# Cross-attention in a decoder layer: where in the slot the scores for a pair of maxima are made

## The reference, cut to what matters

```python
q = (x @ Wq).reshape(B, N, HEADS, hd).transpose(0, 2, 1, 3)
k = (context @ Wk).reshape(B, M, HEADS, hd).transpose(0, 2, 1, 3)
v = (context @ Wv).reshape(B, M, HEADS, hd).transpose(0, 2, 1, 3)
scores = jnp.einsum('bhid,bhjd->bhij', q, k) * scale
scores = jnp.where(context_mask[:, None, None, :], scores, max_neg)
attn = jax.nn.softmax(scores, axis=-1)
out = jnp.einsum('bhij,bhjd->bhid', attn, v)
return out.transpose(0, 2, 1, 3).reshape(B, N, DIM) @ Wo
```

## Time and profile before

| | us |
|---|---|
| median of 3 runs | 3547.63 |
| lowest and highest of them | 3544.5, 3549.58 |
| profiled execution, its own time | 3545.49 |
| its span in the profile | 3543.5 |
| PE busy in the span | 3231.4 |
| DVE busy | 2578.8 |
| ACT busy | 2275.1 |
| POOL busy | 1072.4 |

### The profile page before, as it was taken

How to read it: one execution, slowest core, us unless ns; L and a number is a source line. 1 busy time by engine, 2 the same in 40 slices (tenths; PEclk the granted TensorE clock), 3 DMA queues, 4 the chain that set the end, 5 groups by cost and what they waited for, 6 DMA issues and landing times.

```text
span 3543.5 us, 47102 instructions
## 1 busy us (share of the span) xinstructions
PE 3231.4 (91%) x15056; PEld 2496.3 (70%) x15056; DVE 2578.8 (73%) x4060; ACT 2275.1 (64%) x4138; POOL 1072.4 (30%) x1177
## 2 busy tenths in 40 slices
PE   5999999999999999978999999988989999941998
PEld 4777777777777878755666666655768888831887
DVE  5887877777777777656788787778863369976554
ACT  4776767676666767644777777766432256678765
POOL 1233232333233333343556555557500000000000
PEclk9999999999999999989999999999999999975999
DMA  3443444434334433336666666655722268889764
GB/s 119 159 160 116 125 144 125 128 116 147 119 125 131 134 114 121 105 116 119 105 112 125 118 116 118 124 100 165 237 77 102 107 220 297 294 338 395 271 243 182
DMA packets 269954, 555.47 MB, mean 157 GB/s; under 512 B 28024, under 2 KB 105856, under 8 KB 255376
## 3 DMA queue, kind: packets, MB, share of 16 engines
q1 hardware_dynamic: 265488, 544.08, 52.1%
q10 hardware_dynamic: 4224, 8.39, 0.6%
HBM read 322.72 MB, written 162.30 MB: 137 GB/s over the span
## 4 chain that ended last, share of the span: by engine, by line
PE 40%; DVE 6%; issue 5%; DMA 2%; ACT 1%; POOL 1%; SPq 0%; DVEq 0%; ACTq 0%; POOLq 0%
PE gu_acc L2442 15%; PE ca_mx L2357 3%; DVE ca_negm L1959 3%; PE md_acc L2522 2%; PE md_acc L2524 2%; PE ca_pj L2337 2%; PE md_acc L2523 2%; PE ca_ov L2387 2%; PE ca_ov L2388 2%; PE ca_st L2375 2%; PE ca_pj L2324 2%; DVE ca_el L1974 1%; PE ca_ms L2347 1%; DMA ca_q<-ca_ql 1%; DVE ca_eh L1968 1%
## 5 line engine op out<-in xcount | busy, mean ns | idle before, releaser
L816 POOL TENSOR_SCALAR sa_ex<-sa_ex,sa_rs 128x512 f32<-128x512 f32 x512 | 356.7, 697 | 943.6 <-DVE sa_rs L658 943.6
L653 DVE TENSOR_REDUCE sa_nm<-sa_st 128x1 f32<-128x512 f32 x512 | 351.3, 686 | 261.0 <-PE sa_st L947 259.7
L514 ACT ACTIVATE sa_eh<-sa_tr 128x512 fp32r<-128x512 f32 x512 | 306.8, 599 | 313.6 <-PE sa_tr L957 309.5
L898 PE MATMUL sa_pj<-sa_xh,sa_w 128*128 128x512 f32 x1536 | 457.0, 417 | 2.6 <-DVE sa_xl L631 1.5
L1959 DVE TENSOR_REDUCE ca_negm<-ca_mx 128x2 fp32r<-128x1024 f32 x256 | 312.6, 1221 | 104.4 <-PE ca_mx L2357 100.5
L662 DVE TENSOR_TENSOR sa_el<-sa_tr,sa_eh 128x512 fp32r<-128x512 f32 x512 | 351.5, 687 | 41.0 <-ACT sa_eh L514 34.1
L507 ACT ACTIVATE sa_ex<-sa_st,sa_nm 128x512 f32<-128x512 f32 x512 | 351.0, 686 | 42.0 <-DVE sa_nm L653 38.4
L2231 POOL TENSOR_TENSOR ca_el<-ca_ex,ca_eh 128x512 fp32r<-128x512 f32 x256 | 350.8, 1372 | 62.5 <-ACT ca_eh L1743 62.4
L1735 ACT ACTIVATE ca_ex<-ca_st 128x512 f32<-128x512 f32 x512 | 296.5, 586 | 37.1 <-PE ca_st L2375 35.5
L957 PE MATMUL sa_tr<-top_ident,sa_ex 128*128 128x128 f32 x2048 | 306.5, 272 | 0.7 <-POOL sa_ex L816 0.7
L957 PEld LDWEIGHTS sa_tr<-top_ident,sa_ex 128*128 128x128 f32 x2048 | 254.3, 140 | 72.0 <-POOL sa_ex L816 3.2
(11 more groups left out here) (292 smaller groups left out, 7541.6 us busy)
## 6 DMA issues: line engine op xcount, KB each, us to landing
sa_w<-w_split SPq DMA_DIRECT2D x56, 1536.0 KB, 7.4
gate<-gu_ev SPq DMA_DIRECT2D x24, 1024.0 KB, 4.4
gu_g<-gate SPq DMA_DIRECT2D x48, 512.0 KB, 5.9
gate<-gu_g SPq DMA_DIRECT2D x48, 512.0 KB, 3.6
up<-gu_ev SPq DMA_DIRECT2D x24, 1024.0 KB, 5.7
md_a<-gate SPq DMA_DIRECT2D x96, 256.0 KB, 6.7
md_b<-up SPq DMA_DIRECT2D x96, 256.0 KB, 7.5
md_a<-gate SPq DMA_DIRECT2D x44, 512.0 KB, 15.3
```

What stands on the lines that cost most here:

```text
L514: nc.scalar.activation(eh[:, v % 2], tr[:, v % 2], ACT.Copy).then_inc(act_eh, 1)
L653: nc.vector.tensor_reduce(nm[:, u % U:u % U + 1], st[:, u % 2], AX_X, ALU.max, negate=True).then_inc(dve_mx, 1)
L816: nc.gpsimd.tensor_scalar(ex[:, u % U], ex[:, u % U], rs[:, u % U:u % U + 1], 1.0, ALU.mult, ALU.mult).then_inc(pool_n, 1)
L898: yield nc.tensor.matmul(pj[:, bank], w[:, n % 2, m, part, k], xx[:, b % 2, k], start=(i == 0 and k == 0), stop=(i == 2 and k == DK - 1))
```

## The change

In the loop that issues TensorE's work the two calls for the pair move from behind `scores` to behind the projection passes and the context transposes, ahead of `product`. Nothing else is changed.

```diff
@@ -2460,9 +2460,6 @@
                 n = s + 2
                 if 0 <= G - LA < U * N:
                     scores(G - LA)
-                if 0 <= G + U - LM < U * N and (G - LM) % 2 == 0:
-                    max_scores(G + U - LM)
-                    max_scores(G + U - LM + 1)
                 if t == LM + 1 and 0 <= s < N:
                     max_rows(s)
                 if n < N:
@@ -2487,6 +2484,9 @@
                         issued["value"] += 1
                 if context_tile(s, t) is not None:
                     transpose_context(context_tile(s, t))
+                if 0 <= G + U - LM < U * N and (G - LM) % 2 == 0:
+                    max_scores(G + U - LM)
+                    max_scores(G + U - LM + 1)
                 if 0 <= G - LA - AV < U * N:
                     product(G - LA - AV)
                 if out_slot(G) is not None:
```

## The result

| | before | after |
|---|---|---|
| median of 20 runs each, us | 3547.95 | 3552.34 |
| lowest and highest, us | 3543.47, 3553.54 | 3548.05, 3560.12 |
| profiled execution, its own time, us | 3545.49 | 3549.74 |
| its span, us | 3543.5 | 3547.8 |

What follows compares the result with a forecast made beforehand. No engine is full; PE, busy nine tenths, loses time standing at `ca_mx` for DVE. Gains of 7.4 and 6.4 us, 13.8 off 3545.5, give 3531.7; with 2.1 for the median, 3533.8 us, range 3527 to 3542.

Steps and rivals of the forecast that it cites:

- term 1: Stalls at t = 14 of 14 V groups: product 0.53 us earlier each, 7.4 us gained.
- Terms 1 and 2: PE's stalls at t = 14 of V groups, 7.4 us, and t = 0 after light sections, 13 x 0.49 = 6.4 us.
- Term 3: Entry into light sections: pair of t = 6 0.70 us later, hidden by product and DVE waits; zero, worst 10.5 us.
- Term 4: Heavy slots t = 0 to 7: reduction 0.70 us later, nothing taken; upper bound 31 us.
- rival 2: Slower: DVE's subtraction loses the port to POOL at t = 3, 5, 7, 1.06 us each; 3565, chance 0.04.
- Term 5: Start, group -1: three K passes go ahead of the first pair's DMA wait; zero, bounds 0 and 0.7 us gained.
- Term 6: Granted clock falling to half at 4 of 13 boundaries: zero taken, bounds -5 and +3 us.

Runs made afterwards that it cites:

- e2: The changed kernel, but VectorE makes the values' low part at t = 11 ahead of the reduction; median 3539.0 us, ratio to before 0.9974.
- e5: The kernel before with the pair moved at t = 10 and 12 alone; median 3552.38 us, ratio 1.0011.
- e1: The kernel before with the pair moved at t = 0 and 14 alone; median 3540.07 us, ratio 0.9978.
- e4: The kernel before with the pair moved in all even slots but t = 10 and 12; median 3538.88 us, ratio 0.998.
- f1: The kernel before with the queries' input loaded for the first batch alone; median 3542.4 us, ratio 0.999.
- f2: Pair moved at t = 0 and 14 alone, queries' input loaded for the first batch alone; median 3533.76 us, ratio to before 0.9964.
- c2: The changed kernel again, unchanged, against the kernel before; median 3551.28 us, ratio 1.0011.
- c4: The changed kernel a third time, unchanged, against the kernel before; median 3550.03 us, ratio 1.0008.
- e7: The kernel before with the row of maxima sent from ScalarE's queue instead of SyncE's; median 3550.3 us, ratio 1.0006.
- e6: Pair moved in all even slots but t = 10 and 12, row of maxima sent from ScalarE's queue; 3537.85 us, ratio to before 0.9976.
- c1: The kernel before again, unchanged; median 3548.28 us, ratio 1.0003.
- f3: The changed kernel with the queries' input loaded for the first batch alone; median 3545.19 us, ratio to before 0.9996.

## Why the prediction was wrong

**The step that failed** stands in the change part by part: "Queued behind the moved wait are the product, and the next slot's scores. For those nothing changes in order", and in term 1 the new order "scores 1897.73, two V passes, pair at 1898.43", taken to hold for every slot. I listed what is behind the moved wait and not what moves up ahead of it. The passes have a wait of their own (`bank_free()`), and the pair's place was its cover. At t = 14 that wait is already met, so the slot I worked out had none; at t = 12 it had 0.25 us to spare and lost 0.86. The rows showed it: the low part at 1894.48 for 0.68, the pass at 1895.41. The missing term is 14 x 0.86, about 12.1 us, nearly the whole of the 13.8 forecast; e2 takes the gap away (3.9 us of it come back at the pair), e5 makes it by itself, e1 and e4 are without it.

Nor did I follow the later reduction to the instruction behind it on VectorE. The text did so for the subtraction of t = 11 ("its end stays") and not for the values' low part between the two.

**Terms 1 and 2** came true at their places: 0.55 and 0.51 us by the fences above, for 0.53 and 0.49; 14.5 us in sum for 13.8. In the changed kernel t = 14 alone proves little, since e5 has it without moving that pair; e1 shows that the move does it too, 6.5 of the 7.6 us: there, the wait that I took to be over within 0.01 us is still some 0.07.

**A second shortfall** stands behind the first. Without the gap 7 to 9 us of 13.8 came in (e1, e2, e4). In those profiles 3.4 to 6.2 us more of the stretch than before went into waits for transfers of 8 to 256 KB in the groups that follow a 2 MB load: late next was the row of maxima, which no part of the prediction asks about. The stretches of f1 and f2 fit this: no such waits, and 11.7 us of gain. Their times do not, with 8.6 us. So that these waits make up the second shortfall is argued and not shown.

**Term 3** held. In group 12 the pair of t = 8 starts 0.38 behind the scores in place of 0.23, the product waits for the output bank as before, and the light sections are no longer than they were:

```profile
1943.26 0.73 PE L2357 MATMUL ca_mx<-ca_k,ca_q 97*128 97x512 f32 x2
1944.66 0.42 PE L2387 MATMUL ca_ov<-ca_eh,ca_vc 128*66 128x512 f32 x1 [0.68 <-ACT ca_osb L1749]
```

The stands at that product fell from 13.9 to 11.9 us over the 15 sections, and the pair of t = 8 in the same sections, which had none, has 2.0: the later reduction is hidden by this wait, at no cost and no gain, as forecast.

**Term 4 and rival 2**: it cost TensorE nothing, as taken. Timelines of DVE and POOL, group 10, t = 3 to 7, in the changed kernel:

```profile
1885.48 0.68 DVE L1974 TENSOR_TENSOR ca_el<-ca_ex,ca_eh 128x512 fp32r<-128x512 f32 x1
...
1889.03 1.39 DVE L1974 TENSOR_TENSOR ca_el<-ca_ex,ca_eh 128x512 fp32r<-128x512 f32 x1
1891.14 1.23 DVE L1959 TENSOR_REDUCE ca_negm<-ca_mx 128x2 fp32r<-128x1024 f32 x1 [0.72 <-PE ca_mx L2357]
```

```profile
1885.51 1.80 POOL L2231 TENSOR_TENSOR ca_el<-ca_ex,ca_eh 128x512 fp32r<-128x512 f32 x1 [0.63 <-ACT ca_eh L1743]
...
1888.58 1.30 POOL L2216 TENSOR_TENSOR ca_kl<-ca_km,ca_kh 128x512 fp32r<-128x512 f32 x1 [1.26 <-ACT ca_kh L1711]
1889.84 1.07 POOL L2224 TENSOR_SCALAR ca_eh<-ca_ex 128x512 fp32r<-128x512 f32 x1
```

At t = 3 DVE began 0.03 ahead and POOL's took 1.80 for its usual 1.29; at t = 5 DVE began 0.45 behind and took 1.39 for 0.68. The idle 0.72 before the next reduction took that, so no pair was late.

**Term 5**: the first groups gained nothing; the three profiles of the changed kernel took 71.3 to 73.5 us from the first context transpose to group 1, the two of before 70.9 and 73.2. **Term 6**: 13.7 us of the stretch at 1.2 GHz in both profiles of before, 0.0, 6.8 and 3.4 in three of the changed one. It is not the same from one execution to the next. The medians owe next to nothing to it: the mean granted clock over the runs is 0.9672 in c2 and 0.9669 in c4, against 0.9673 and 0.9668 in the kernel before beside them.

**What stays open.** By stands the changed kernel should be level: -14.5 and +12.1, and +3.8, +0.7 or +1.8 for DMAs in its three profiles. The time says 2.9 to 4.4 us slower, and the clock of the runs does not carry that. The stretches can be freed of the clock. In each of the 14 profiles, the stretch less its stands at full clock and less half of its time at 1.2 GHz is 646.0 to 646.6 us, with 0.0 to 13.7 us at 1.2 GHz among them, so time at 1.2 GHz costs half of itself here. With that half taken off, the two profiles of before have 721.5 and 721.8 us, and the three of the changed kernel 724.0, 722.3 and 723.7. So freed of the clock, the changed stretch is 0.5 to 2.5 us longer and not 4.3 shorter. The two figures of before are rather too low, because TensorE also stood in part of its slow time there, and a stand costs the same at either clock; e7, with TensorE's order of before and 3.4 us at 1.2 GHz, has 723.9. Level to 2 us longer is what the stretches bear out. Among the kernels that ran together and have the same 3.4 us at 1.2 GHz, stretch and median agree in direction: against e7 (725.6, 3550.3) c4 has -0.2 and -0.3 us, e5 +2.2 and +2.1, e6 -15.1 and -12.5. Behind the stretch, from the scores of group 30 to the last transpose of the output (L2415), the changed kernel took 197.0, 196.6 and 196.8 us against 194.0 and 195.7, but e4, which gains 9 us, has 196.8 and e1 199.6, so this is no finding. Where the last 1 to 4 us of the loss lie stays open.

## What to carry to other kernels

When an instruction with a wait is moved behind others, ask two questions, not one: what is queued behind it, and which wait of those that now move up it had been covering, by how many ns of slack. Follow each producer that comes later as a result down its own engine to the instruction behind it, and hold that one's end against its consumer's new due time. And work the new order out for every slot of the period, not only for those in which there is a wait today: the loss here came in a slot that had none.

## What was not expected of the hardware

- A wait on a semaphore can stand in the profile as "issue". The 14 gaps of t = 12 were VectorE's `dve_vl`, as e2 shows, and neither of their rows (14.6 us at the weight loads of the stretch, 8.9 at the matmuls) names an engine:

```profile
PEld ca_ms L2347 <- issue: 14.6, 14, 1.0
```

- VectorE's subtraction and GpSimd's held each other up in both directions. Waiting behind one of GpSimd's it did go in between two that follow each other without idle time: the one of 1889.03 above ended at 1890.42, and GpSimd's next instruction, the cast of 1889.84 (`ca_kl` ended at 1889.88), took 1.07 us for its median 0.63. GpSimd's mean over 256 subtractions rose from 1372 ns (1368 in c1) to 1487, 1468 and 1466 in the three profiles of the changed kernel. VectorE's went from 932 in both profiles of before to 915, 944 and 946. So the reorder brought more contention, and most of it fell on the engine with time to spare. The Trainium skill, "SBUF — State Buffer", section "SBUF: two separate sides", has it that whichever starts first keeps the pair and the other blocks; the trace agrees in the main: GpSimd's 1.80 us and VectorE's 1.39 are each 0.14 less than the rest of the other's instruction and their own usual time (0.65 + 1.29, 0.85 + 0.68).
- An 8 KB row of maxima, issued from SyncE's queue 5.2 us ahead of the time when the scores were due, kept TensorE waiting for up to 2.0 us behind 2 MB of input (e4); issued as early from ScalarE's queue, the longest wait there was 0.7 (e6). Without the loads (f1 to f3) there was no such wait. But ScalarE's queue is not the faster one as such: in groups 30 and 31 the row sent from it came 2.1 us late, and from SyncE's it did not.
